# Fifth layer of a six-layer kernel: weigh ahead of the next projection, x normed on ScalarE

## The reference, cut to what matters

```python
def _layernorm(x, axis=-1, eps=1e-05):
    m, v = mean(x), var(x)
    return (x - m) / sqrt(v + eps)

q, k, v = proj(Wq, bq), proj(Wk, bk), proj(Wv, bv)
scores = einsum('bhqd,bhkd->bhqk', q, k) / sqrt(hd)
truth_penalty = sigmoid(truth_gate) * (norm(k, keepdims) * 0.01)
entropy = -sum(exp(logp) * logp)            # logp = log_softmax(scores)
balance_adjustment = sigmoid(balance_gate) * (entropy / log(S) * 0.1)
order_bonus = sigmoid(order_gate) * (position_bias * 0.05)
justice_adjustment = sigmoid(justice_gate) * ((mean_score - scores) * 0.1)
harmony_smooth = sigmoid(harmony_gate) * (smoothness * 0.1)
scores = scores - truth_penalty + balance_adjustment + order_bonus \
         + justice_adjustment + harmony_smooth
out = einsum('bhqk,bhkd->bhqd', softmax(scores), v)
return out @ Wo.T + bo
```

## Time and profile before

| | us |
|---|---|
| median of the runs | 2546.84 |
| the profiled execution | 2551.28 |
| its span | 2549.1 |
| TensorE busy | 2021.6 (79%) |
| vector engine busy | 1869.5 (73%) |
| ScalarE busy | 1400.2 (55%) |
| GpSimd busy | 474.1 (19%) |

### The profile page before, as it was taken

One profiled execution on the slowest core, in us unless ns is written; L12 is line 12 of the kernel. 1 busy time (PEld: TensorE's weight loads), 2 busy tenths in 40 slices (PEclk: granted clock), 3 DMA queues, 4 the chain that ended last, 5 costly groups with the idle time before them and its releaser, 6 DMA issues.

```text
span 2549.1 us, 51234 instructions
## 1 busy us (share of the span) xinstructions
PE 2021.6 (79%) x15447; PEld 1440.2 (56%) x15486; DVE 1869.5 (73%) x5158; ACT 1400.2 (55%) x3709; POOL 474.1 (19%) x561
## 2 busy tenths in 40 slices
PE   4689999999999688565799999999866756665655
PEld 4667777777776555232566766667655543333332
DVE  3348888778787456798577787877457768888887
ACT  1035655555655243453366656666545647776775
POOL 0011122111121000010243343333134430000000
PEclk9999999999999799676899999999978777899998
DMA  2001111111110200200012112111010000000000
GB/s 97 0 15 30 30 32 29 29 29 29 30 32 16 80 1 1 92 1 34 13 47 63 55 50 63 54 38 30 18 28 11 10 8 1 0 0 0 0 0 33
DMA packets 64759, 71.83 MB, mean 28 GB/s; under 512 B 40402, under 2 KB 42131, under 8 KB 63636
## 3 DMA queue, kind: packets, MB, share of 16 engines
q1 hardware_dynamic: 64660, 70.73, 9.3%
HBM read 63.47 MB, written 2.10 MB: 26 GB/s over the span
## 4 chain that ended last, share of the span: by engine, by line
PE 58%; DVE 23%; issue 9%; ACT 8%; DVEq 1%; DMA 1%; SPq 0%; POOL 0%; ACTq 0%; POOLq 0%
PE ps L645 5%; PE ps L616 5%; PE ps L607 4%; PE ps L629 3%; PE ps L677 3%; PE ps L1831 3%; PE ps L1814 3%; PE ps L579 3%; PE ps L1771 2%; PE ps L1761 2%; PE ps L2194 2%; PE ps L1840 2%; DVE f_ams L2505 2%; PE ps L1796 2%; DVE d_ks L1613 2%
## 5 line engine op out<-in xcount | busy, mean ns | idle before, releaser
L362 ACT ACTIVATE a_pr<-ps,a_nm 128x257 f32<-128x257 f32 x512 | 238.1, 473 | 183.1 <-DVE a_nm L476 183.1
L1563 ACT ACTIVATE d_pr<-d_st,d_nm 128x257 f32<-128x257 f32 x256 | 128.2, 502 | 207.4 <-DVE d_nm L1683 197.8
L484 DVE COPY a_pT<-ps 128x512 f32<-128x512 f32 x256 | 170.3, 686 | 92.7 <-PE ps L645 92.1
L2578 PE MATMUL ps<-f_wt,f_nxT 128*128 128x512 bf16 x481 | 150.1, 436 | 68.4 <-DVE f_act L2489 63.1
L476 DVE TENSOR_REDUCE a_nm<-ps 128x2 f32<-128x514 f32 x256 | 174.4, 681 | 0.0
L645 PE MATMUL ps<-ident,a_pr 128*128 128x128 f32 x1024 | 160.4, 279 | 0.0
L1814 PE MATMUL ps<-d_kc,d_qc 128*128 128x257 f32 x512 | 147.2, 412 | 0.0
L645 PEld LDWEIGHTS ps<-ident,a_pr 128*128 128x128 f32 x1024 | 117.5, 141 | 33.4 <-issue 12.7
L607 PE MATMUL ps<-a_cT,a_wqk 128*128 128x257 f32 x512 | 133.2, 382 | 2.9 <-DVE a_k L450 1.7
L302 POOL TENSOR_TENSOR a_sf<-a_sf,a_ratio 128x256 f32<-128x256 f32 x64 | 39.4, 616 | 507.0 <-DVE a_ratio L505 507.0
L616 PE MATMUL ps<-a_wvg,a_cT 128*128 128x256 f32 x512 | 129.4, 396 | 0.0
(11 more groups left out here) (350 smaller groups left out, 5313.9 us busy)
## 6 DMA issues: line engine op xcount, KB each, us to landing
a_cT<-in_ctx SPq DMA_DIRECT2D x64, 257.0 KB, 2.7
d_cT<-in_ctx SPq DMA_DIRECT2D x64, 257.0 KB, 2.8
f_wf<-in_f_w SPq DMA_DIRECT2D x24, 512.0 KB, 3.7
a_vbd<-a_vself SPq DMA_DIRECT2D x256, 8.0 KB
e_vb<-e_vs SPq DMA_DIRECT2D x256, 8.5 KB
c_wf<-in_c_w SPq DMA_DIRECT2D x3, 1024.0 KB, 7.1
x_all<-in_x SPq DMA_DIRECT2D x1, 2048.0 KB, 8.0
d_wo<-in_d_wo SPq DMA_DIRECT2D x1, 2048.0 KB
```

Of the source, the lines that this page charges most:

```text
L362: ins = act.activation(pr[j][:, g, :], ps[:, S_BANK[u % 2] + k, S:LK], ACT.Exp, bias=nm[j][:, g:g + 1], accum_out=ssum[j][:, 0, g:g + 1])
L484: dve.tensor_copy(pT[u][:, :, :, :], ps[:, T_BANK[u % 2], :].rearrange("p (g c q) -> p g c q", g=2, c=2))\
L1563: ins = act.activation(pr[j][:, g, :], st[u][:, k, :], ACT.Exp, bias=nm[u][:, k:k + 1], accum_out=sm[j][:, g:g + 1])
L2578: ins = pe.matmul(ps[:, 2 + 2 * k + w, :], lhsT=nxT[s][:, c, :], rhs=wt[:, 3 * e + w, c * IE:c * IE + IE], start=(c == 0), stop=(c == KT - 1))
```

## The change

Two edits in `gated_attention`. On TensorE, `weigh(t-1)` stands ahead of `project(t+1)`. And x is normed on ScalarE, as scale times x plus shift with scale = rstd and shift = -mean x rstd, where the shifts of all 16 tiles are made in one vector instruction at the start; `normal(t+2)` stands behind `turned(t+1)` in ScalarE's step. Since the vector engine's steps are now alike, its last two go into its loop; ScalarE's loop is one turn shorter, with two steps written out.

```diff
+        shift = sb("e_shift", [P, NT])
...
         def scalar(act):
...
+            def normal(t, first=False):
+                if not first:
+                    act.wait_ge(xT_psum.sem, xT_psum.at(t, 0))
+                act.activation(xn[:, :], x_all[:, t, :], ACT.Identity, bias=shift[:, bass.ds(t, 1)],
+                               scale=rstd_all[:, bass.ds(t, 1)]).then_inc(xn_ready.sem, 1)
...
-            def step(t, j, pair, prev=True, more=True):
+            def step(t, j, pair, prev=True, more=True, more2=True):
                 if more:
                     turned(t + 1)
+                if more2:
+                    normal(t + 2)
                 if prev:
                     shares(t - 1)
...
+            normal(0, True)
             turned(0)
+            normal(1)
             queries_keys(0)
...
-            with act.Fori(0, NT // 2 - 1) as i:
+            with act.Fori(0, NT // 2 - 2) as i:
                 step(i * 2 + 1, 1, i + 1)
                 step(i * 2 + 2, 0, i + 1)
-            step(NT - 1, 1, NT // 2, more=False)
+            step(NT - 3, 1, NT // 2 - 1)
+            step(NT - 2, 0, NT // 2 - 1, more2=False)
+            step(NT - 1, 1, NT // 2, more=False, more2=False)
...
         def vector(dve):
...
             norm_vector(dve, n)
+            dve.scalar_tensor_tensor(shift[:, :], mv_all[:, :, 0], -1.0, rstd_all[:, :], ALU.mult, ALU.mult)\
+                .then_inc(bias_ready.sem, 1)
             dve.wait_ge(sig_done.sem, sig_done.at(0, 1))
-
-            def normal(t, first=False):
-                if not first:
-                    dve.wait_ge(xT_psum.sem, xT_psum.at(t, 0))
-                normed(dve, xn[:, :], t).then_inc(xn_ready.sem, 1)
-
-            normal(0, True)
-            normal(1)
...
-                if more2:
-                    normal(t + 2)
...
-            with dve.Fori(1, NT - 2) as t:
+            with dve.Fori(1, NT) as t:
                 step(t)
-            step(NT - 2, more2=False)
-            step(NT - 1, more=False, more2=False)
...
         def tensor(pe):
...
                     turn_x(t + 1)
-                    project(t + 1)
                 if prev:
                     weigh(t - 1, 1 - j, pair)
                 if more:
+                    project(t + 1)
                     project_v(t + 1)
```

More of the change, by code:

```diff
@@ L1931, in gated_attention @@
         r2 = sb("e_r2", [P, NH])
+        shift = sb("e_shift", [P, NT])
         w_loaded = shared("w_loaded", 16 * 10, 1)
-        sig_done, zeroed, bias_ready = signal("e_sig_done"), signal("e_zeroed", 5), signal("e_bias_ready", 2)
+        sig_done, zeroed, bias_ready = signal("e_sig_done"), signal("e_zeroed", 5), signal("e_bias_ready", 3)
         yb_psum, yb_ready = signal("e_yb_psum"), signal("e_yb_ready")
@@ L2120, in added, with step @@
                 add_to_x(dve, n, t, ps[:, Y_BANK, 0:HID])
-            def step(t, prev=True, more=True, more2=True):
+            def step(t, prev=True):
                 link.at(t)
```

## The result

The changed kernel takes 2586.78 us, the median of 4 runs (2582.76 to 2587.25), against 2545.45 us for the kernel before in runs taken beside it (4 runs). The ratio is 1.0156, 95% interval 1.0135 to 1.0177: slower, by 41 us in the medians, where 30 were forecast. The two profiled executions are 36 us apart: 2587.25 against 2551.28 us, with spans of 2585.4 and 2549.1.

A forecast was written before the change was run, and what follows sets the result against it. It took the vector engine's chain to bound the kernel, with project to Ln to f 0.3 us behind and deciding afterwards: 14 x 2.1 = 29.5, plus 0.5 and 0.4, is 30.4 us more, 2577 us (2556 to 2598).

The forecast's parts named there:

- f to the start of xnT: Term of the new period, from vector row f to the copy xnT: 2.65 us, mean of 2.98 and 2.32.
- project's end to f: Term of the new period over e_kx, project_v, table load, Ln: 6.80 us plus 0.46 for the lower clock.
- Weigh ahead of project: TensorE order: the 1.91 us wait before e_r goes, but project starts later by pT's copy, normal and weigh.
- the sign that was named for the mechanism: Vector engine: new idle time before T2, waiting for Ln, 3 us or more; without it the mechanism is wrong.
- the second reading decides the forecast: The chain project, e_kx, project_v, Ln, f runs some 0.3 us behind the first; delays to project are paid in full.
- the projection at the full clock: Rival, chance 0.13: project takes 2.1 us right behind weigh; period 13.1 us, 2539 us, or some 2548 with half the steps.
- if project takes near 2 us: Sign on TensorE that the forecast is wrong; it had taken 3.5 us for project, mostly at the lower clock.
- x normed on ScalarE: ScalarE: normal takes 0.60 us, puts 0.50 us between xnT and pT, plus 0.1 us for register instructions.
- Whatever shortens the vector engine's work earns at most 0.3 us a tile: Vector engine: gain capped because the chain over project and Ln is only 0.3 us behind.
- The lower clock: TensorE: clock follows its busy share, falling to 0.62; half of project_v's extra 0.93 us was taken, 0.46.
- Ends of the layer: First normal and the last two vector steps outside the repeated periods: 0.5 and 0.4 us more.
- TensorE mostly at its lower clock: Rival, chance 0.22: idle time keeps TensorE slow, project 3.77 us; period 17.1 us, 2595 us.

The follow-up runs named there:

- e4: The changed kernel with Ln right behind the first Exp on ScalarE, ahead of the next tile's queries, keys and values: 2585.10 us, ratio 1.0150.
- e7: The changed kernel with unread TensorE products added, two in the wait for pT and three in the wait for the keys: 2555.87 us, ratio 1.0028.
- e2: The changed kernel with the TensorE reorder undone, so only x normed on ScalarE against the kernel before: 2531.36 us, ratio 0.9935.
- e8: e2 with two unread products of 128x256 on TensorE between weigh and project_v: 2545.68 us, ratio 0.9990 to the kernel before.
- e10: The changed kernel with unread products only in TensorE's wait for pT (two of 128x240): 2560.11 us, ratio 1.0061.
- e11: The changed kernel with unread products only in TensorE's wait for the keys (three of 128x256): 2568.09 us, ratio 1.0087.

## Why the prediction was right, point by point

The time lies in the range and the sign held, with a share of luck: the path that was to close the period did not, and two terms that were off by 0.90 and 0.56 us nearly cancel. The sum was 11 us short of the medians' difference, 6 us short of the profiled executions' (30.4 against 36.0). The terms of the period, as means over the periods to tiles 1 to 13, beside what was taken:

| term | taken | measured | before |
|---|---|---|---|
| f to the start of xnT | 2.65 | 3.55 | 2.68 |
| xnT to weigh | 1.52 | 1.46 | |
| weigh | 0.9 | 0.99 | 0.68 |
| project | 3.5 | 2.94 | 3.49 |
| project's end to f | 7.26 | 7.21 | 7.12 |

- *Weigh ahead of project* turned the wait before e_r into later waits, as forecast: the vector engine waits 49.5 us for Ln, the sign that was named for the mechanism. But **the chain project, project_v, Ln, f does not close the period**, as the prediction had it ("the second reading decides the forecast"): e4 takes Ln out of it, and the period stays (16.27 us). TensorE's own queue closes it, from project through output to the next transposes. That project's end to f is 7.21 us, nearly the 7.26 taken, did fit because the two chains lie so close: the exponential of f is there some 0.65 us in the mean before TensorE is through with output.
- So the term that was too small is **f to the start of xnT**, "mean 2.65": it assumed that the transposes start as soon as the exponential of f is there. They start 2.06 us after f instead of 1.41, for at the lower clock output is not done. With the transposes themselves at the lower clock in most steps the term is 0.90 us too small. In e7 the transposes start 1.41 us after f again.
- *Project* was taken 0.56 us too long: the clock rises within it earlier than before, and in 4 of 14 steps project runs wholly at the full clock, in 2.05 us. That is the condition of the rival *the projection at the full clock*, and the prediction's own sign of being wrong ("if project takes near 2 us"). This rival was thus true in part, in a kernel that became slower all the same, since the clock that project gained the rear part of the step lost.
- *x normed on ScalarE*: 0.589 us against 0.60, and 0.49 us between xnT and pT against 0.50. Right in size; the 0.1 us for register instructions, an assumption, were 0.04. That its cost in the new order is 1.20 us a tile (16.08 against 14.88), not 0.6, is the clock.
- "Whatever shortens the vector engine's work earns at most 0.3 us a tile" was wrong. It was read from one step, that of tile 14, with project at the lower clock. e2 earns 0.96 us. Its direct part, 0.38 us from project's end to f, is near the 0.3; the larger part is where the full clock falls in the shorter step, of which the prediction took no account. For the sum of this change it did no harm.
- *The lower clock*, taken at half of its price for project_v: the direction was right (0.80 to 0.65 from 1900 to 2040 us), but not the reading that the clock follows TensorE's share of busy time. The earlier trace rows has a share of 0.71 with a clock of 0.81; the stretch 2000 to 2040 of the changed kernel has 29.73 us of 40, a share of 0.74, with a clock of 0.63. The same products take longer at the lower clock, so the share does not fall to the 0.62 of the prediction. The price too was larger than that one term: all of TensorE's tail is longer, and 1.9 us a tile go when the gaps are filled.
- *Ends of the layer*: f of tile 0 lies 26.45 us behind the statistics, against 26.12 before, 0.3 us for 0.5 taken. The last period costs 1.67 us, where 0.4 was taken; for 1.2 us of it the transposes of the probabilities are to blame, which stand behind an output at the lower clock and end 3.28 us after f instead of 2.07.
- The rival *TensorE mostly at its lower clock* (2595 us) was as near in time as the forecast (2577): 8 us off, the forecast 10. The profile lies between: output was at the lower level in all steps, as this rival would have it, but project took 2.94 us in the mean and not its 3.77.

## What to carry to other kernels

Work that waits for a copy, put ahead of work that is ready, makes everything behind it in the queue pay the wait, here with TensorE's clock on top. Before pricing an engine's wait as a gain, follow the chain that is second, and as a third the engine's own queue once around the loop at the lower clock; here it was this third one that closed the period. Try the parts of a change apart: the norm on ScalarE earns 15 us alone and costs 1.2 us a tile only behind the new order on TensorE.

## What the runs showed of the hardware that was not expected

- Work that nobody reads made a kernel faster: e7 holds five products more per tile than the changed kernel and is 31 us faster, at a clock of 0.84 instead of 0.65. The same trick in another order (e8) made it 14 us slower at 0.82 instead of 0.80, so the mean clock of a stage does not tell the time; which instructions get the full clock does. e10 and e11 say the same: e11 has the higher clock (0.78 against 0.73) and the longer period (15.39 against 14.41 us), with project at 3.50 us in the mean against 2.08.
- How long some GpSimd instructions take hangs on what the vector engine does beside them and on which started first. The product kk takes 1.04 us in the changed kernel and mostly 1.27 before. It is not e_xn that does this: before, kk ends 0.1 us ahead of it (1961.85 + 1.27 against 1963.20 us). It is the product u (line 2138, read from SBUF like kk): wherever u is already running when kk starts, in all 14 traces, kk takes 0.90 us plus the time that the two overlap: 1.27 with 0.37, 1.45 with 0.55.
- GpSimd's square root of 16 values takes 3.36 us where the vector engine's subtraction for w1 (e_w, line 2128) is already running when it starts, as in all steps before, and 2.91 where it starts first, as in 14 of the 16 of the changed kernel. The subtraction takes 0.88 us in the first case and 0.69 in the second. So it is in all 14 traces.
- e_xn of the kernel before, 0.75 instead of 0.41 us in 13 of 16 tiles, starts in just these tiles 0.12 us behind GpSimd's addition of the output bias to x.
